# A macaron block with a selective scan: the LayerNorm roots of the mixer split over two engines, the first FFN's statistics and normalisation moved to other slots, x loaded a period sooner, and the beginning in another order

## The chip, the cores and the metric

The kernel runs on one core of a Trainium2 chip. The metric is the device time of one execution in microseconds; the median of three runs is given. A profile is of one execution, and its times are microseconds from the start of its span.

## What is computed

x has 32 sequences of 256 tokens with 128 channels. Three sublayers follow each other, each on a LayerNorm of x:

```python
x = x + 0.5 * ffn(layernorm(x))
x = x + mixer(layernorm(x))
x = x + 0.5 * ffn(layernorm(x))

def ffn(x):                      # E = 8 experts, top 1
    logits = xf @ Wg + bg
    idx = argmax(softmax(logits))
    h = gelu(einsum('th,ehi->tei', xf, W1) + b1)
    y = einsum('tei,eih->teh', h, W2) + b2
    return y[idx]

def mixer(x):                    # selective scan, D_IN = 256, N = 16
    xn = x * rsqrt(mean(x*x) + 1e-6) * norm_w
    x_path, z_path = split(xn @ in_proj_w.T)
    x_path = silu(causal_conv4(x_path))
    dt_x, B, C = split(x_path @ x_proj_w.T)
    dt = softplus(dt_x @ dt_proj_w.T + dt_proj_b)
    h[t] = exp(dt * A) * h[t-1] + dt * x_path * B
    y = sum_n h * C + D * x_path
    return (y * silu(z_path)) @ out_proj_w.T + x
```

The mixer adds its own input, the LayerNorm of x, as a residual, and takes an RMS norm of that same LayerNorm. In the kernel the two norms are one step on the moments: with variance v, the RMS-normed value is (x - mean) times (v (1 + 1e-6) + 1e-11) to the power -1/2, and the residual update is x (1 + r) - mean r, with r = (v + 1e-5) to the power -1/2.

## The kernel before

The tokens are worked on in 16 chunks of 512 (two sequences). A program of 21 iterations, -4 to 16, runs over them as a software pipeline. An iteration has 16 slots, and in iteration i each engine works on several chunks: the state scan of chunk i, the dt path of chunk i+1, the mixer's norm and the end of the first FFN of chunk i+2, the first products of the first FFN of chunk i+3, the statistics of chunk i+4, and the second FFN of chunks i-1 to i-3. The order within an iteration is written by hand in `Plan` tables: for each engine, at which slot a named step is issued (a half or a quarter means behind the slot's units). Iterations 0 to 15 follow `STEADY`; -4 to -1 follow the `FILL` tables, 16 follows `DRAIN`. Each engine runs its own queue in order, and semaphores order the engines among each other.

The state scan has 32 units in a period, two for each slot. For a unit ScalarE writes the decay exp(dt A) into one of three PSUM banks dA0 to dA2 (`make_decay`, L882), GpSimd multiplies dtx by B (`state_bx`, L1253, two units at once), VectorE scans (L1050, L1052), and the product with C is made by VectorE (L1056) or, for half of the units, by GpSimd (`product_c`, L1263). A decay waits until the unit three before it has left its bank. TensorE sums the states (`sum_states`, L656) in the odd slots and in slot 0 of the next iteration. `gated0` and `gated1` on VectorE (L1129) multiply the sums by the gate.

An FFN chunk is a transposed normalised input (`ln_f1`, `ln_f2`), a gate product (`gate_f1`), a one-hot by VectorE (`one_hot`), its transposition (`oh_f1`), eight first products e0 to e7 into the bank PH (two of them into PY), copied out by ScalarE (L830, L827), two batched gelus (L852) with a table load on either side, and eight second products into PY (L644). VectorE adds the result to x (`y_f1`, `y_f2`, L1109).

A norm is made of `norm_stats` on VectorE (`stats_f1`, `stats_f2`, `stats_p`; L1031 to L1037), the root, and the application. In `STEADY` the root is `root_*` on ScalarE: Ln and then Exp with a factor -0.5, from the same table as the decays (L798, L800; for the mixer both roots at once, L807 to L811), while GpSimd's `root_*` negates the mean, waits for ScalarE and makes the shift. In `FILL` GpSimd takes the roots itself as a power (L1211, L1230). `norm_f1` and `norm_f2` on ScalarE apply the norm in four pieces (L789); `norm_p` on GpSimd makes xr (L1241), which TensorE transposes (`ln_p`); `res_p` on ScalarE updates x (L817). SP issues all transfers: `x_in` loads chunk i+4 at slot 5 in `STEADY`, right behind the store of chunk i-3 (`x_out`), and ahead of the store of the B and C rows (`bc`). X has room for eight chunks.

## Time and profile before

| | us |
|---|---|
| median of three runs | 1206.37 (1206.27 to 1208.4) |
| profiled execution | 1208.04 |
| its span | 1206.1 |
| busy in the span: TensorE, GpSimd, VectorE, ScalarE | 1045.0, 1008.1, 1003.7, 924.9 |

The page of the profile gives busy times and the chain of work that ended last; in the order of time that chain shows a beginning up to 94 us, a stretch in which GpSimd's products follow each other up to 190, periods of some 68 us, and from 995 again GpSimd, until an end without a scan from about 1157. To read such a kernel, take one period of it as windows and then as a timeline of each engine: the number in brackets is how long the engine stood before an instruction, and who released it.

### The profile page before, as it was taken

To read this page: it belongs to the slowest core of one execution; us is meant where nothing else is said; L and a number is where in the kernel's file an instruction comes from. 1 tells how busy PE (TensorE), PEld (TensorE's weight loads), DVE (VectorE), ACT (ScalarE), POOL (GpSimd) and SP (SyncE) were. 2 spreads that over 40 slices of the span, in tenths; PEclk is the share of its full clock that TensorE was granted. 3 is DMA by queue.
4 is the path that set the end of the run, shared out by engine and by line. 5 is a ranking of instruction groups with operands and counts; after the bars stand their busy time and mean duration, and the time that the engine had idled before them with its cause. 6 is when DMAs were issued, how large, how long until landed. Compare 5 with 4: busy or idle time off the path is not lost.

```text
span 1206.1 us, 16727 instructions
## 1 busy us (share of the span) xinstructions
PE 1045.0 (87%) x5380; PEld 544.9 (45%) x5380; DVE 1003.7 (83%) x1638; ACT 924.9 (77%) x1440; POOL 1008.1 (84%) x628
## 2 busy tenths in 40 slices
PE   6896959798989999998989999898989997958688
PEld 3452425253535454453534454453544454524246
DVE  2236999998999899898989899899989899999851
ACT  2367687878989797988989797988989787685551
POOL 1129999988999899998999899998999999999920
PEclk9797979898999899998999899998999998988699
DMA  4033434324142424325143424315142423334000
GB/s 104 1 111 146 140 114 143 113 80 168 29 166 98 149 88 159 105 80 185 30 152 111 145 93 140 125 63 189 43 149 98 148 98 138 118 116 140 9 9 18
DMA packets 61751, 130.05 MB, mean 108 GB/s; under 512 B 7552, under 2 KB 28720, under 8 KB 53472
## 3 DMA queue, kind: packets, MB, share of 16 engines
q1 hardware_dynamic: 61664, 128.98, 31.5%
q8 instruction: 43, 0.70, 0.2%
...
## 4 chain that ended last, share of the span: by engine, by line
PE 42%; ACT 17%; POOL 15%; DVE 13%; issue 11%; DMA 1%; SPq 0%; DVEq 0%; POOLq 0%; ACTq 0%
PE PY L644 12%; POOL hb L1253 9%; PE PH L611 9%; PE G L592 6%; DVE dA L1052 5%; ACT hs L852 5%; POOL hb L1263 4%; PE Y L656 4%; DVE hb L1050 3%; ACT dA L882 3%; PE PH L610 3%; ACT hs L830 2%; DVE hb L1056 2%; PE dA L624 2%; PE G L715 1%
## 5 line engine op out<-in xcount | busy, mean ns | idle before, releaser
L1253 POOL TENSOR_TENSOR hb<-dtx_rep,bs 128x1024 f32<-128x1024 f32 x256 | 598.1, 2358 | 17.6 <-PE Y L656 16.1
L882 ACT ACTIVATE dA<-dt_rep,A 128x512 f32<-128x512 f32 x512 | 341.5, 689 | 96.5 <-DVE hb L1056 87.0
L1052 DVE TENSOR_TENSOR_SCAN dA<-dA,hb 128x512 f32<-128x512 f32 x272 | 331.5, 1219 | 8.3 <-DVE oh L1094 3.0
L1050 DVE TENSOR_TENSOR_SCAN hb<-dA,hb 128x512 f32<-128x512 f32 x240 | 279.0, 1206 | 28.2 <-ACT dA L882 28.0
L1263 POOL TENSOR_TENSOR hb<-hb,cs 128x1024 f32<-128x1024 f32 (+1 forms) x128 | 283.1, 2222 | 10.3 <-DVE hb L1050 10.1
L644 PEld LDWEIGHTS PY<-W,hs 128*128 128x128 f32 x2048 | 248.5, 193 | 64.8 <-issue 61.6
L644 PE MATMUL PY<-W,hs 128*128 128x128 f32 x2048 | 260.9, 280 | 0.0
L611 PE MATMUL PH<-xnT,W 128*128 128x512 f32 x396 | 231.8, 668 | 0.0
L1056 DVE TENSOR_TENSOR hb<-dA,cs 128x512 f32<-128x512 f32 x272 | 188.1, 692 | 19.8 <-DVE dA L1052 0.5
L830 ACT COPY hs<-PH 128x512 f32<-128x512 f32 x198 | 115.2, 582 | 95.1 <-PE PH L611 79.5
L656 PE MATMUL Y<-hb,Sel 128*32 128x512 f32 x1024 | 149.7, 655 | 37.3 <-POOL hb L1263 34.8
L610 PE MATMUL PH<-ohT,Lm 24*128 24x512 bf16 x198 | 77.9, 393 | 64.4 <-ACT hs L830 64.4
L852 ACT ACTIVATE hs<-hs 128x2048 f32<-128x2048 f32 x54 | 103.1, 1915 | 0.3
L610 PEld LDWEIGHTS PH<-ohT,Lm 24*128 24x128 bf16 x198 | 18.0, 91 | 157.6 <-ACT hs L830 121.1
L1069 DVE SCALAR_TENSOR_TENSOR xs<-G,Wc,xs 128x506 f32<-128x506 f32 (+2 forms) x96 | 66.7, 737 | 25.7 <-ACT xs L914 23.2
L611 PEld LDWEIGHTS PH<-xnT,W 128*128 128x128 f32 x396 | 60.8, 193 | 46.6 <-issue 46.6
L1279 POOL TENSOR_TENSOR dt<-dt,sp 128x1024 f32<-128x1024 f32 x16 | 37.9, 2367 | 44.8 <-ACT sp L942 44.7
L656 PEld LDWEIGHTS Y<-hb,Sel 128*32 128x32 f32 x1024 | 22.4, 111 | 103.6 <-issue 69.5
L592 PE MATMUL G<-xs,Wxdt 128*128 128x512 f32 x128 | 58.7, 602 | 1.0 <-DVEq L1098 1.0
L789 ACT ACTIVATE xn<-X,shift,rstd 128x128 f32<-128x128 f32 x124 | 50.8, 482 | 5.0 <-POOL shift L1213 5.0
L715 PE MATMUL G<-Wg,xnT 128*128 128x8 f32 x256 | 37.0, 271 | 18.7 <-ACT xnT L778 17.7
L715 PEld LDWEIGHTS G<-Wg,xnT 128*128 128x128 f32 x256 | 34.2, 208 | 37.1 <-ACT xnT L778 37.1
...
## 6 DMA issues: line engine op xcount, KB each, us to landing
...
bs<-bc_rows SPq DMA_DIRECT2D x64, 256.0 KB, 3.8
cs<-bc_rows SPq DMA_DIRECT2D x64, 256.0 KB, 3.7
dtx_rows<-dtx SPq DMA_DIRECT2D x32, 256.0 KB, 2.5
dt_rows<-dt SPq DMA_DIRECT2D x32, 256.0 KB, 2.6
X<-in_x SPq DMA_DIRECT2D x16, 256.0 KB, 3.1
out<-X SPq DMA_DIRECT2D x16, 256.0 KB, 2.4
```

Source lines behind the costliest of these rows:

```text
L610: nc.tensor.matmul(bank[:, :], Lm[:, e, :], ohT[:, w, (it.i0 + off) % 2, :], start=True, stop=False)
L611: nc.tensor.matmul(bank[:, :], W1[:, e, :], xnT[:, w, :], start=False, stop=True).then_inc(full, 1)
L644: last = nc.tensor.matmul(PY[:, P * j:P * (j + 1)], hs[:, w, e, P * j:P * (j + 1)], W2[:, e, :], start=False, stop=e == E - 1 and j == J - 1)
L656: last = nc.tensor.matmul(Y[D32 * g:D32 * (g + 1), :], Sel[:, :], hb[:, (2 * k + g // 2) % HR, g % 2], start=k == 0, stop=q == NQ - 1)
L830: nc.scalar.copy(hs[:, w, e, :], PH[:, :]).then_inc(ph_free, 1)
L852: nc.scalar.activation(a, a, ACT.Gelu).then_inc(gelu[w], 1)
L882: nc.scalar.activation(dA[u % NA][:, :], dt_rep[:, h, g, :], ACT.Exp, scale=A[:, h, g, q:q + 1]).then_inc(decay, 1)
L1050: nc.vector.tensor_tensor_scan(x_in_hb, a, x_in_hb, 0.0, ALU.mult, ALU.add).then_inc(scan, 1)
L1052: nc.vector.tensor_tensor_scan(a, a, x_in_hb, 0.0, ALU.mult, ALU.add).then_inc(scan, 1)
L1056: nc.vector.tensor_tensor(x_in_hb, a, cs[:, q, :], ALU.mult).then_inc(prod, 1)
L1253: nc.gpsimd.tensor_tensor(hb[:, s % HR], dtx_rep[:, h, 2 * m:2 * m + 2, :], bs[:, q, None, :].broadcast_to([P, 2, CH]), ALU.mult).then_inc ...
L1263: nc.gpsimd.tensor_tensor(h_in_hb, h_in_hb, cs[:, q, None, :].broadcast_to([P, n, CH]), ALU.mult) \
```

## The change

`STEADY` and three `FILL` tables get other slots, and the roots of the mixer's norm are divided.

- The second products of the first FFN go from slots 5, 6, 6, 7, 7, 8, 8, 8 to 5, 6, 7, 7, 8, 8, 9, 9. `y_f1` moves from slot 9.5 to 10.0, behind the same `gated0`, and `stats_p` from 10.0 to 10.5, behind units 20 and 21. The copy of first product e5 moves from slot 11 to directly behind the second gelu of the second FFN, ahead of the table load.
- The root for the RMS norm is taken by GpSimd alone (`inverse_root_p`: one operation for the argument and a power), so `norm_p` waits for no other engine. The root for the residual stays with ScalarE, as one Ln and one Exp at slot 11.5 instead of three instructions at 10.5, ahead of the gelus; GpSimd turns it into scale and shift in a new step `res_p` at slot 12.0, for which ScalarE's `res_p` now waits.
- `stats_f1` goes from slot 12 of VectorE to 1.25, `root_f1` from 12.5 to 4.5 on ScalarE and to 6.5 on GpSimd, `norm_f1` from 14.5 to 9.0 on ScalarE. For this x of chunk i+5 is loaded at slot 5, where chunk i+4 was; the load now waits for the store of chunk i-3, issued just before it.
- In the beginning three second products of chunk 0 stand behind the transposes and around the gate of chunk 1, the one-hot copy of chunk 1 ahead of `y_f1` of chunk 0, and the steps of iteration -2 one slot earlier; `res_p` and `norm_f1` there stand behind `taps`. Iteration -1 loads two chunks of x.

```diff
-    w2=[*[(0, e, s, 1, 2) for e, s in experts(5, 6, 6, 7, 7, 8, 8, 8)],
+    w2=[*[(0, e, s, 1, 2) for e, s in experts(5, 6, 7, 7, 8, 8, 9, 9)],
...
-         "ln_f2": 9.5, "root_p": 10.5, "gelu_f2": 10.5, "ln_p": 12.5,
-         "root_f1": 12.5, "res_p": 13.5, "taps": 14.0, "norm_f1": 14.5, "gelu_f1": 15.5},
+         "ln_f2": 9.5, "gelu_f2": 10.5, "root_p": 11.5, "ln_p": 12.5,
+         "res_p": 13.5, "taps": 14.0, "gelu_f1": 15.5},
...
             def scale_residual(it, off):
                 it.wait(act, xr_ready, off, 1, 1)
+                it.wait(act, rooted[2], off, 1, 1)
...
                     if it.has(off):
                         a = hs[:, w, 4 * k:4 * (k + 1)].rearrange("p e t -> p (e t)")
                         nc.scalar.activation(a, a, ACT.Gelu).then_inc(gelu[w], 1)
+                    take_units(it, s, 3 + k)
                     if k == 0:
-                        take_units(it, s, 3)
...
+            def inverse_root_p(it, off):
+                n = roots_before(2, it.i0 + off)
+                it.wait(pool, moments[2], off, 1, 1)
+                it.wait(pool, normed[2], off, 1, 0)
+                nc.gpsimd.tensor_scalar(neg[:, 2, :], mv[:, 2, :, 0], -1.0, 0.0, ALU.mult, ALU.add).then_inc(pool_ln[2], 1)
+                nc.gpsimd.tensor_scalar(var[:, :], mv[:, 2, :, 1], 1.0 + RMS_EPS, RMS_EPS * LN_EPS, ALU.mult, ALU.add) \
+                    .then_inc(pool_ln[2], 1)
+                pool.wait_ge(pool_ln[2], n + 2)
+                nc.gpsimd.tensor_tensor(rms[:, :], var[:, :], half[:, :], ALU.pow).then_inc(pool_ln[2], 1)
+
+            def residual_scale(it, off):
+                n = roots_before(2, it.i0 + off) + 3
                 if root_on_act(2, it.i0 + off):
                     pool.wait_ge(log_root[2], 2 * act_roots(2, it.i0 + off) + 2)
...
+                nc.gpsimd.tensor_scalar(res[:, :], rstd[:, 2, :], 1.0, 1.0, ALU.mult, ALU.add)
+                nc.gpsimd.tensor_tensor(shift[:, 2, :], neg[:, 2, :], rstd[:, 2, :], ALU.mult).then_inc(rooted[2], 1)
...
             def normalize_p(it, off):
-                it.wait(pool, rooted[2], off, 1, 1)
+                pool.wait_ge(pool_ln[2], roots_before(2, it.i0 + off) + 3)
...
-            def load_x(it):
-                dst, src = X[:, it.tiles(4), :], xd[:, J * (it.i0 + 4):J * (it.i0 + 5), :]
-                it.wait(sp_, x_out, 4 - XR, 16, 16)
+            def load_x(it, off):
+                dst, src = X[:, it.tiles(off), :], xd[:, J * (it.i0 + off):J * (it.i0 + off + 1), :]
+                it.wait(sp_, x_out, off - XR, 16, 16)
```

On ScalarE, slots 9 and 10 of a steady iteration (decays 20 to 23 are those into dA2, dA0, dA1, dA2), before:

```order
L830 COPY hs<-PH 128x512
L882 ACTIVATE dA2<-dt_rep,A 128x512
L882 ACTIVATE dA0<-dt_rep,A 128x512
L778 COPY xnT<-G1 128x512
L830 COPY hs<-PH 128x512
L882 ACTIVATE dA1<-dt_rep,A 128x512
L882 ACTIVATE dA2<-dt_rep,A 128x512
L807 ACTIVATE var<-mv,eps 128x4
L808 ACTIVATE var<-mv,eps_p 128x4
L811 ACTIVATE roots<-var 128x8
L852 ACT_TABLE_LOAD
```

and with the change:

```order
L790 ACTIVATE xn<-X,shift,rstd 128x128 x4
L821 COPY hs<-PH 128x512
L873 ACTIVATE dA2<-dt_rep,A 128x512
L873 ACTIVATE dA0<-dt_rep,A 128x512
L779 COPY xnT<-G1 128x512
L821 COPY hs<-PH 128x512
L873 ACTIVATE dA1<-dt_rep,A 128x512
L873 ACTIVATE dA2<-dt_rep,A 128x512
L843 ACT_TABLE_LOAD
```

The normalisation of the first FFN now stands ahead of the copy of first product e1, and nothing stands between decay 23 and the table load of the gelus.

On VectorE, slots 9 to 11 of the same iteration (the scans with dA2 and dA0 behind the addition to x are units 20 and 21), before:

```order
L1129 TENSOR_TENSOR y2<-Y,zs 128x512 [waits summed]
L1109 SCALAR_TENSOR_TENSOR X<-PY,X 128x512 [waits w2_done_f1]
L1031 BN_STATS stat<-X 128x6 [waits moments_p,y_added_f1]
L1031 BN_STATS stat<-X 128x6 x3
L1035 COPY ticket<-ticket 128x1 [waits normed_p,stats_p]
L1037 BN_AGGR mv<-stat 128x2 x4
L1052 SCALAR_TENSOR_TENSOR dA2<-dA2,hb 128x512 [waits bx,decay]
L1056 TENSOR_TENSOR hb<-dA2,cs 128x512 [waits scan,c1_in]
L1050 SCALAR_TENSOR_TENSOR hb<-dA0,hb 128x512 [waits decay]
```

and with the change:

```order
L1119 TENSOR_TENSOR y2<-Y,zs 128x512 [waits summed]
L1099 SCALAR_TENSOR_TENSOR X<-PY,X 128x512 [waits w2_done_f1]
L1042 SCALAR_TENSOR_TENSOR dA2<-dA2,hb 128x512 [waits bx,decay]
L1046 TENSOR_TENSOR hb<-dA2,cs 128x512 [waits scan,c1_in]
L1040 SCALAR_TENSOR_TENSOR hb<-dA0,hb 128x512 [waits decay]
L1021 BN_STATS stat<-X 128x6 [waits moments_p,y_added_f1]
L1021 BN_STATS stat<-X 128x6 x3
L1025 COPY ticket<-ticket 128x1 [waits normed_p,stats_p]
L1027 BN_AGGR mv<-stat 128x2 x4
```

The statistics for the mixer moved behind units 20 and 21; the other statistics, of the first FFN, stood behind the one-hot copy of slot 12 and now stand behind the one-hot steps of slot 1.

On TensorE in the beginning, between the last first products of chunk 0 and the first ones of chunk 1, before:

```order
L644 MATMUL PY<-W2,hs 128x128 x3
L584 MATMUL G0<-Id,xn 128x128 [waits g0_free,normed_f1]
L584 MATMUL G0<-Id,xn 128x128 x3
L715 MATMUL G1<-Wg,xnT 128x8 [waits g1_free,g0_free]
L715 MATMUL G1<-Wg,xnT 128x8 x3
L724 MATMUL G1<-Idb,oh 24x128 [waits g1_free,gate_f1]
L724 MATMUL G1<-Idb,oh 24x128 x3
L623 MATMUL PH<-ohT,Lm 128x512 [waits direct_done,g1_free]
```

and with the change:

```order
L585 MATMUL G0<-Id,xn 128x128 x3
L645 MATMUL PY<-W2,hs 128x128 [waits direct_done]
L645 MATMUL PY<-W2,hs 128x128 x3
L716 MATMUL G1<-Wg,xnT 128x8 [waits g1_free,g0_free]
L716 MATMUL G1<-Wg,xnT 128x8 x3
L645 MATMUL PY<-W2,hs 128x128 [waits direct_done]
L645 MATMUL PY<-W2,hs 128x128 x3
L645 MATMUL PY<-W2,hs 128x128 [waits direct_done]
L645 MATMUL PY<-W2,hs 128x128 x3
L725 MATMUL G1<-Idb,oh 24x128 [waits g1_free,gate_f1]
L725 MATMUL G1<-Idb,oh 24x128 x3
L624 MATMUL PH<-ohT,Lm 128x512 [waits direct_done,g1_free]
```

Three second products, four matmuls each, now stand between the transposes, the gate product and the transposed one-hot.

## Rows read from the trace of the kernel before

**Rows 1.** windows: stretch, length, busy us (count) by engine, TensorE clock, DMA share, GB/s

```profile
40.00:60.00 20.00, 15.86 (x35) 5.85 (x35) 6.10 (x31) 6.03 (x12) 5.98 (x14) 0.66 0.00 0
385.13:453.86 68.73, 63.88 (x337) 33.63 (x337) 62.27 (x102) 59.00 (x93) 62.41 (x39) 0.95 0.35 117
453.86:521.75 67.89, 61.34 (x337) 32.64 (x337) 62.34 (x102) 58.99 (x93) 62.34 (x39) 1.00 0.34 118
```

**Rows 2.** GpSimd's timeline: start us, us, instruction; first and last dt sum

```profile
189.81 2.37 POOL L1279 TENSOR_TENSOR dt<-dt,sp 128x1024 f32<-128x1024 f32 x1
...
1006.60 2.37 POOL L1279 TENSOR_TENSOR dt<-dt,sp 128x1024 f32<-128x1024 f32 x1 [0.87 <-ACT sp L942]
```

**Rows 3.** VectorE's timeline, period of full clock; in brackets idle before, releaser

```profile
472.43 0.69 DVE L1129 TENSOR_TENSOR y<-Y,zs 128x512 f32<-128x512 f32 x1 [0.71 <-PE Y L656]
...
473.76 0.87 DVE L1031 BATCH_NORM_STATS2 stat<-X 128x6 f32<-128x128 f32 x4
...
484.01 0.41 DVE L1105 COPY ohT<-G 24x512 bf16<-24x512 bf16 x1 [0.46 <-PE G L724]
...
486.90 2.34 DVE L1050 TENSOR_TENSOR_SCAN hb<-dA,hb 128x512 f32<-128x512 f32 x2 [1.23 <-ACT dA L882]
...
511.02 3.45 DVE L1050 TENSOR_TENSOR_SCAN hb<-dA,hb 128x512 f32<-128x512 f32 x3 [0.67 <-ACT dA L882]
```

**Rows 4.** timeline of ScalarE in the same period

```profile
471.46 0.59 ACT L830 COPY hs<-PH 128x512 f32<-128x512 f32 x1 [3.12 <-PE PH L611]
...
477.05 0.69 ACT L882 ACTIVATE dA<-dt_rep,A 128x512 f32<-128x512 f32 x1 [2.04 <-DVE hb L1056]
477.68 0.28 ACT L807 ACTIVATE var<-mv,eps 128x4 f32<-128x4 f32 x1
...
478.40 1.28 ACT L852 ACT_TABLE_LOAD   x1
...
489.12 0.29 ACT L798 ACTIVATE vt<-mv,eps 128x4 f32<-128x4 f32 x1
489.44 0.20 ACT L800 ACTIVATE rstd<-vt 128x4 f32<-128x4 f32 x1
...
496.39 1.65 ACT L789 ACTIVATE xn<-X,shift,rstd 128x128 f32<-128x128 f32 x4
...
499.89 0.69 ACT L882 ACTIVATE dA<-dt_rep,A 128x512 f32<-128x512 f32 x1 [1.39 <-DVE hb L1056]
```

**Rows 5.** timeline of TensorE in the same period

```profile
466.72 2.84 PE L644 MATMUL PY<-W,hs 128*128 128x128 f32 x24
...
482.14 0.39 PE L610 MATMUL PH<-ohT,Lm 24*128 24x512 bf16 x1 [2.36 <-ACT hs L830]
```

**Rows 6.** timeline of GpSimd in the same period

```profile
462.15 2.37 POOL L1279 TENSOR_TENSOR dt<-dt,sp 128x1024 f32<-128x1024 f32 x1 [1.25 <-ACT sp L942]
...
478.54 0.19 POOL L1220 TENSOR_SCALAR neg<-mv 128x4 f32<-128x4 f32 x1
...
479.34 1.75 POOL L1241 TENSOR_SCALAR xr<-X,neg,roots 128x128 f32<-128x128 f32 x4
...
489.72 0.20 POOL L1213 TENSOR_TENSOR shift<-neg,rstd 128x4 f32<-128x4 f32 x1 [2.60 <-ACT rstd L800]
```

**Rows 7.** timeline of TensorE in the beginning

```profile
40.50 1.06 PE L715 MATMUL G<-Wg,xnT 128*128 128x8 f32 x8 [0.68 <-ACT xnT L778]
43.21 0.38 PE L724 MATMUL G<-Idb,oh 128*24 128x128 bf16 x4 [1.65 <-DVEq L1098]
45.58 0.60 PE L623 MATMUL PH<-ohT,Lm 24*128 24x512 bf16 x1 [1.99 <-DVE ohT L1105]
46.12 2.08 PE L624 MATMUL PH<-xnT,W 128*128 128x512 f32 x2
```

**Rows 8.** timeline of GpSimd in the beginning: the power of 128x4

```profile
50.61 1.01 POOL L1211 TENSOR_TENSOR rstd<-vt,half 128x4 f32<-128x4 f32 x1
```

**Rows 9.** section 6 of the page, DMA issues: count, KB each, us to landing

```profile
out<-X SPq DMA_DIRECT2D x16, 256.0 KB, 2.4
```

More of the change, by code:

```diff
@@ L225, in roots_before @@
 def roots_before(w, chunk):
-    return sum(1 if root_on_act(w, c) else 4 if w == 2 else 3 for c in range(chunk))
+    return sum((2 if w == 2 else 0) + (1 if root_on_act(w, c) else 3) for c in range(chunk))
 def on_pool(s):
@@ L547, in body @@
                             store_x(it, off)
[L548 to L549 removed]
+                    for t, off in at.get("x_in", ()):
+                        if t == s and it.has(off):
+                            load_x(it, off)
                     if not it.has(1):
```

97 lines of the change are left out of this document (40 added, 57 removed).

## The prediction

> **What bounds the kernel now.** I read the stretches first [rows 1]. In the steady part no engine is full: of 67.89 us in one period VectorE is busy 62.34, GpSimd 62.34, TensorE 61.34 and ScalarE 58.99. Periods come in pairs, one of about 68.7 us with a granted clock of 0.95 and one of 67.9 at 1.00; twelve of them, from the dt sum of GpSimd at 189.81 to the one at 1006.60 [rows 2], take 816.8 us, 68.07 each. So the period is a ring of waits that runs through several engines, and a change is worth what it takes out of that ring. I follow it in the period of full clock. TensorE hands the state sum to VectorE (`gated0`, which waited 0.71 us) [rows 3]; VectorE adds the FFN to x, takes the statistics for the mixer (`stats_p`) and only then scans unit 20. ScalarE waits 2.04 us for that unit's product before it may write decay 23, then computes three small roots, 477.68 to 478.40, loads a table and runs the gelus [rows 4]. TensorE stands 2.36 us until the gelu lets ScalarE free PH [rows 5]; VectorE stands 1.23 us at 486.90 for the next decay [rows 3]. From there VectorE is the late one (ScalarE waits 1.39 us for it at 499.89), until the gelus of the first FFN, after which VectorE waits 0.67 us for decay 3. GpSimd follows with waits of 1.25 and 2.60 us [rows 6].
>
> **Slots 7 to 11.** Of the eight second products of the first FFN, two now stand behind the state sum of slot 9 on TensorE. Three of them take 2.84 us [rows 5], so the sum comes 1.9 us sooner; it is ready before VectorE is, and VectorE's 0.71 goes. The eighth product still ends where the old sum ended, so `y_f1` can start right behind `gated0`, some 0.7 earlier than before. `stats_p` (0.87 + 0.15 + 0.37 us with overlaps, 1.26 from 473.76 to 475.02) moves from ahead of unit 20 to behind unit 21. Unit 20's product is then 0.7 + 1.3 = 2.0 to 2.1 us earlier, and decay 23 with it: I take 2.1, all of the 2.04 plus gaps, since decay 22 is ready then. The roots of ScalarE, 0.72, no longer stand between decay 23 and the gelus. The gelus start 2.8 us earlier. Two things must keep up, and just do: `e5` of TensorE needs the sum of slot 11, for which GpSimd's product ends at 478.5 as before, and its copy now stands ahead of the table load behind the second gelu, which wants it at about 481.8; by the same durations it is ready at 481.5.
>
> **The split roots.** GpSimd computes the root of the normalised input itself: one more small operation (0.19) and one power. I price the power from the beginning, 1.01 us for 128x4 [rows 8], so 1.2 a period, ends 1.0 and 1.6. The neg-to-xr stretch, 0.80 now [rows 6], grows to about 1.7; against it the 2.60 us that GpSimd stood for ScalarE's root_f1 goes, because that root now runs at slot 6.5 behind root_f2. The residual's root is taken by GpSimd at slot 12: it needs ScalarE's Ln and Exp, which stand behind the table reload and two decays; they end about 485.0, GpSimd arrives about 485.3. GpSimd's own ring is the 62.34 busy and 1.2, 63.5 to 64.1 with gaps; it stays under the period. Its transposed input is needed by TensorE 2.7 us after it is ready even so, hence the later `stats_p` costs nothing there.
>
> **First FFN's statistics and normalisation.** `norm_f1`, 1.65 us at 496.39, goes to slot 9, where ScalarE waited 3.12 us at 471.46 for TensorE [rows 4]. That wait is 1.9 shorter by the moved products, so 1.2 of the 1.65 are hidden and 0.4 fall on ScalarE, which has them spare before decay 23. What leaves slot 14 buys nothing in this period, since ScalarE waits for VectorE right behind it (the 1.39). `stats_f1` leaves slot 12, where VectorE waited anyway (0.46 and 1.23) [rows 3], and lands in slot 1.25, 1.26 us ahead of a wait of 0.67: that costs 0.6 on the ring. root_f1 on ScalarE adds 0.49 (0.29 + 0.20) ahead of softplus, so GpSimd's dt sum gains 2.36 instead of 2.85, still more than the ring.
>
> **Sum of a period.** -2.1 - 0.7 + 0.6 = -2.2: 67.9 becomes 65.7. A check from the other side: VectorE waited 0.71, 0.46, 1.23 and 0.67, together 3.1; without them its queue alone asks 64.8, and I leave it 0.9 of waits. The slower of each pair of periods had the lower level of TensorE's clock (1.2 instead of 2.4 GHz in part), and it fell at the 2.4 us stand behind the gelu. That stand shrinks below 0.7. I therefore let all periods run at full clock, so 68.07 becomes 65.7: 12 x 2.37 = **-28.4 us**; bounds 2.2 less by 1.2 (a late `e5`) and the VectorE floor of 64.8, -14 and -39.
>
> The Trainium skill ("TensorE: Matmul & The Clock Gate", Part 1, "What's actually happening") says that "the default state is throttled, and activity releases the throttle". By that rule a denser stream keeps the clock. The trace agrees in that the clock of the period was 0.95 or 1.00 with the same stand of 2.36 us, so a stand of that size can go either way; if the rule gave nothing here, the sum would keep 0.4 us a period.
>
> **The x load.** It is issued one period sooner and now waits for the landing of the store issued just before it, 2.4 us [rows 9]; behind it in SP's queue stands the store of the B and C rows. These rows are read more than 20 us later, so the cost is nil; if that cover were gone it would be 1.5 us a period.
>
> **Beginning.** TensorE idled 0.68 + 1.65 + 1.99 = 4.3 us between the FFN of chunk 0 and that of chunk 1 [rows 7]. Transposes and gate of chunk 1 now lie between the last second products, and the copy of the one-hot stands ahead of `y_f1`; about 0.7 is left, so 3.6 are won. After that stand TensorE ran at the lower clock (0.66 over 40 to 60) [rows 1]: a pair of 2.08 us would be half that. Five pairs and small ones, some 6 us, could come back. Against it ScalarE now does residual and normalisation, twice 1.65 us as in [rows 4], late in that iteration, ahead of the copy of the combined weights for which TensorE waits. The whole comes to between -3.5 and -9; I take **-6**. GpSimd then bounds the first two periods and the one behind the last FFN: +1.2 for two of them that lie outside the twelve, and +0.5 for ScalarE's root ahead of the first dt sum: **+2.9**.
>
> **Total.** -28.4 - 6 + 2.9 = -31.5. The profiled execution took 1208.04 us with a span of 1206.1; its work is that of the median run, 1206.37, within 0.15%, so I subtract from the median: **1174.9**.
>
> **Rivals.** (a) *`e5` ends last.* Sum of slot 11, PH copy, `e5`, its copy: this line has 0.3 us to spare, and it carries GpSimd's product, 16.4 us of work behind the dt sum. If it is 1 us late, the table reload and decay 24 are too, one for one: 12 x 1 = 12, 1187. For it speaks that I have placed some forty waits to 0.1 us; against it that dt itself comes sooner. (b) *The clock still falls* once a period, or in every other one, at a smaller stand: 0.4 to 0.8 a period, 5 to 10 us, 1182. (c) *Only the beginning gains*, because another wait takes the 2.1 us of decay 23, for instance the copy of `e2`, whose matmuls now stand behind two second products; then the 0.6 of slot 1 eats most of the rest: between 1200 and 1206. (d) *Slower.* The same, with the price of VectorE in full: if the gelus start less than 0.6 us sooner, `stats_f1` in slot 1 costs 0.6 a period and gives nothing back in slot 12, which ScalarE limited; and of the 0.49 of root_f1 on ScalarE some 0.3 reach the ring. 12 x 0.9 + 2.9 - 6 = +8: 1214. Against (c) and (d): the 2.04 us is the plainest wait of the period and what stood ahead of it, `stats_p`, is really moved. That the change does not do what it says is no rival here: the order of the instructions shows each move.
>
> **Chances.** Forecast 0.58, (a) 0.15, (b) 0.13, (c) 0.06, (d) 0.08. The range 1167 to 1190 holds the forecast with its bounds, (a) and (b) for the most part. A measurement of this kernel can tell about 0.2% (2.4 us) from no change: faster 0.88, same 0.04, slower 0.08.
>
> **What would show it.** In the steady part: ScalarE's wait for VectorE ahead of decay 23 under 0.6 us; TensorE's stand behind the first gelu under 0.8; no wait of GpSimd ahead of `shift`; a clock of 1.00 in all periods; dt sums 65.7 apart; VectorE no longer idle for decay 3. Right in kind but not in size would be dt sums 64.8 to 67 apart. In the beginning: first products of chunk 1 at 42 instead of 45.6, half as long, and the first `hb` of GpSimd at 88 instead of 94. Wrong would be a period above 67.5, or a new wait of ScalarE for TensorE in slots 10 and 11.

## The result

| | before | after |
|---|---|---|
| median, us | 1206.32 (1205.49 to 1208.40, 4 runs) | 1176.25 (1171.48 to 1177.37, 4 runs) |
| profiled execution | 1208.04 | 1177.37 |
| its span | 1206.1 | 1175.6 |

The ratio is 0.9741, with an interval of 0.9711 to 0.9771: faster by 30 us, where 31.5 were forecast. The two profiled spans are 30.5 us apart, and the sum below is made against that number.

Two rows of the page of the profile after: busy us, share of the span and instructions of each engine, and TensorE's clock in 40 slices of the span, in tenths of full speed:

```profile
PE 1027.6 (87%) x5380; PEld 543.8 (46%) x5380; DVE 1000.0 (85%) x1637; ACT 920.9 (78%) x1426; POOL 1025.1 (87%) x658
...
PEclk9996979799999999999999999999999998979699
```

GpSimd is busy 17 us more than before, by the powers (about 1.0 us for each of 16 chunks), and TensorE 17 us less with the same number of matmuls, 5380: it ran fewer of them at the lower clock (mean clock 0.949 for 0.937).

GpSimd's timeline after, the two dt sums that answer to [rows 2] (start us, us):

```profile
183.25 2.37 POOL L1275 TENSOR_TENSOR dt<-dt,sp 128x1024 f32<-128x1024 f32 x1
...
975.60 2.36 POOL L1275 TENSOR_TENSOR dt<-dt,sp 128x1024 f32<-128x1024 f32 x1 [0.67 <-ACT sp L933]
```

The sixteen dt sums cut the span into pieces that can be compared one by one:

| piece | before | after | difference | forecast |
|---|---|---|---|---|
| start to first dt sum | 81.12 | 72.51 | -8.6 | -6 |
| two intervals bound by GpSimd | 45.82, 62.87 | 46.74, 64.00 | +0.9, +1.1 | with the last one +2.9 |
| twelve periods | 816.79 | 792.35 | -24.4 | -28.4 |
| interval behind them | 62.57 | 63.47 | +0.9 | (in the +2.9) |
| last dt sum to the end | 136.93 | 136.53 | -0.4 | 0 |

Windows after (stretch, length, busy us and count by engine, TensorE's clock, DMA share, GB/s). The first answers to the first of [rows 1], the second is the first of the twelve periods, the others are steady ones:

```profile
40.00:60.00 20.00, 17.30 (x40) 5.75 (x40) 8.02 (x29) 13.16 (x23) 6.45 (x15) 0.91 0.00 1
183.25:252.30 69.05, 60.80 (x280) 27.05 (x273) 61.16 (x101) 52.27 (x87) 63.55 (x42) 0.90 0.32 112
450.05:515.89 65.84, 61.28 (x339) 32.83 (x338) 61.93 (x102) 58.64 (x92) 63.57 (x41) 1.00 0.36 121
581.71:647.77 66.06, 62.48 (x339) 33.59 (x338) 61.92 (x102) 58.95 (x92) 63.53 (x40) 0.97 0.36 121
```

A period of full clock went from 67.89 us [rows 1] to 65.83, where 65.7 was forecast. All but two of the periods behind the first have a clock of 1.00; those two read 0.97 and are 0.2 longer. Before, every other period from the third on read 0.95 and was 0.8 longer. Of the twelve periods only the first got longer: 69.05 against 66.93, with a clock of 0.90 for 0.95.

### The steady period after

ScalarE's timeline after, in the period that begins at 450.05 (start us, us, instruction; in brackets idle before, releaser). It answers to [rows 4]:

```profile
461.89 0.59 ACT L821 COPY hs<-PH 128x512 f32<-128x512 f32 x1 [1.90 <-PE PH L612]
462.37 1.44 ACT L873 ACTIVATE dA<-dt_rep,A 128x512 f32<-128x512 f32 x2
463.83 1.28 ACT L843 ACT_TABLE_LOAD   x1
465.13 1.91 ACT L843 ACTIVATE hs<-hs 128x2048 f32<-128x2048 f32 x1
...
485.31 0.69 ACT L873 ACTIVATE dA<-dt_rep,A 128x512 f32<-128x512 f32 x1 [2.46 <-DVE hb L1046]
```

The wait of 2.04 us before decay 23 is gone: decays 22 and 23 are one group, 1.44 us long where a pair without a wait takes 1.30, and the table load follows directly. What stands ahead of them is new, a wait of 1.90 us for the matmuls of first product e2.

VectorE's timeline after, answering to [rows 3]:

```profile
460.46 0.69 DVE L1099 SCALAR_TENSOR_TENSOR X<-PY,X 128x512 f32<-128x512 f32 x1 [0.27 <-PE PY L645]
...
462.40 0.69 DVE L1046 TENSOR_TENSOR hb<-dA,cs 128x512 f32<-128x512 f32 x1
...
472.32 2.34 DVE L1040 TENSOR_TENSOR_SCAN hb<-dA,hb 128x512 f32<-128x512 f32 x2 [1.14 <-ACT dA L873]
...
497.25 3.42 DVE L1040 TENSOR_TENSOR_SCAN hb<-dA,hb 128x512 f32<-128x512 f32 x3
```

The wait before `y2` (0.71) and the 0.67 for decay 3 are gone, and 1.14 for decay 24 stands where 0.46 and 1.23 stood. Unit 20's product ends at 463.09, just as decay 23 is to start, and the copy of e2 with decay 22 behind it, which waited for TensorE, is done at about 463.0: VectorE and TensorE's matmuls of e2 now hold ScalarE back to within 0.1 us of the same time.

TensorE's timeline after, answering to [rows 5]. The first row is the one behind the copy for which TensorE stood 2.36 us before; the last row stands 38 us later, just behind the silus:

```profile
467.62 0.39 PE L611 MATMUL PH<-ohT,Lm 24*128 24x512 bf16 x1
...
473.93 0.38 PE L642 MATMUL PY<-b_part,ohT 24*128 24x128 bf16 x4 [1.36 <-issue]
...
505.73 0.38 PE L611 MATMUL PH<-ohT,Lm 24*128 24x512 bf16 x1 [0.99 <-ACT hs L821]
```

The stand of 2.36 us behind the first gelu is gone, and so are the slow matmuls that followed it in every other period before (pairs of 2.08 us at 413.94 and 417.02, behind a stand of 2.37 us). In the two periods that still read 0.97 the slow matmuls follow the stand of 1.36 us. Read the last row with the period before it: from such a stand (439.9) to 466.2, for 26 us, TensorE has only one wait, of 0.33 us. GpSimd, answering to [rows 6], has 0.92 before its dt sum at 515.89 and 0.55 for TensorE at 504.48, and none ahead of `shift`; it is busy 63.57 of 65.84.

### The profile page after: what moved, and what is told of

Its sections match the earlier page's. It is cut to its first block, busy times and chain, and to the rows that moved or that the text cites. A ratio compares the mean times of both kernels' runs of the same rounds, so it can differ in the third digit from the quotient of the medians.

```text
span 1175.6 us, 16745 instructions
## 1 busy us (share of the span) xinstructions
PE 1027.6 (87%) x5380; PEld 543.8 (46%) x5380; DVE 1000.0 (85%) x1637; ACT 920.9 (78%) x1426; POOL 1025.1 (87%) x658
## 3 DMA queue, kind: packets, MB, share of 16 engines
q1 hardware_dynamic: 61664, 128.98, 32.1%
## 4 chain that ended last, share of the span: by engine, by line
PE 31%; POOL 20%; DVE 18%; ACT 18%; issue 12%; DMA 1%; SPq 0%; DVEq 0%; POOLq 0%; ACTq 0%
POOL hb L1247 10%; PE PY L645 10%; DVE dA L1042 7%; PE PH L612 6%; POOL hb L1257 6%; DVE hb L1040 5%; ACT dA L873 4%; PE Y L657 4%; ACT hs L843 3%; DVE hb L1046 3%; PE G L593 3%; ACT hs L821 2%; DVE xs L1059 2%; PE PH L611 2%; PE dA L625 1%
## 5 line engine op out<-in xcount | busy, mean ns | idle before, releaser
L645 PEld LDWEIGHTS PY<-W,hs 128*128 128x128 f32 x2048 | 252.3, 195 | 75.5 <-issue 72.3
L645 PE MATMUL PY<-W,hs 128*128 128x128 f32 x2048 | 268.0, 283 | 0.0
L612 PE MATMUL PH<-xnT,W 128*128 128x512 f32 x396 | 226.4, 654 | 0.0
L1021 DVE BATCH_NORM_STATS2 stat<-X 128x6 f32<-128x128 f32 x192 | 41.3, 278 | 12.6 <-DMA X<-in_x 9.9
```

The costliest lines, as they stand in the source:

```text
L612: nc.tensor.matmul(bank[:, :], W1[:, e, :], xnT[:, w, :], start=False, stop=True).then_inc(full, 1)
L645: last = nc.tensor.matmul(PY[:, P * j:P * (j + 1)], hs[:, w, e, P * j:P * (j + 1)], W2[:, e, :], start=False, stop=e == E - 1 and j == J - 1)
```

## The experiments

Each kernel is the changed one but for the edit shown; e5 is the kernel before with a part of the change. Times are the medians, ratios are to runs of the kernel before that were taken on the same chip (medians 1204.60 for e0, e2, e4 and e6, 1206.29 for e1, e3, e5 and e7, 1205.96 for e8 to e11), so between these sets the ratios compare better than the times. "Full clock" is the most common length of a period with a clock of 1.00 (e8 has nearly none, see there), "twelve" the sum of the twelve periods in the profiled execution, of which the first alone differs by up to 4 us with TensorE's clock.

In the text, an e with a number is an experiment, unless it stands with first products, copies, matmuls or a bank, where it is the expert.

| kernel | median, us | ratio, interval | first dt sum | full clock | twelve |
|---|---|---|---|---|---|
| before | 1206.3 | | 81.12 | 67.90 | 816.8 |
| the change | 1176.25 | 0.9741 (0.9711 to 0.9771) | 72.51 | 65.83 | 792.4 |
| e0, the change once more | 1174.63 | 0.9745 (0.9723 to 0.9767) | 73.90 | 65.85 | 789.2 |
| e1, beginning of before | 1183.99 | 0.9804 (0.9775 to 0.9834) | 81.44 | 65.83 | 792.3 |
| e2, first FFN's norm back | 1176.74 | 0.9760 (0.9738 to 0.9783) | 72.62 | 65.52 | 790.8 |
| e3, second products back | 1180.15 | 0.9782 (0.9758 to 0.9806) | 72.42 | 66.27 | 794.1 |
| e4, `stats_p` ahead of unit 20 | 1192.77 | 0.9889 (0.9869 to 0.9909) | 74.77 | 67.20 | 804.8 |
| e5, split roots alone | 1207.80 | 1.0016 (0.9998 to 1.0033) | 75.67 | 67.70 | 818.9 |
| e6, `stats_f1` in slot 12 | 1176.12 | 0.9766 (0.9740 to 0.9791) | 70.56 | 65.84 | 792.7 |
| e7, power taken twice | 1179.29 | 0.9778 (0.9753 to 0.9802) | 74.21 | 65.83 | 791.5 |
| e8, `root_p` ahead of the gelus | 1198.19 | 0.9936 (0.9922 to 0.9950) | 74.37 | (68.04 at 0.97) | 812.8 |
| e9, e5's copy later | 1182.55 | 0.9807 (0.9792 to 0.9823) | 73.37 | 65.76 | 795.5 |
| e10, e7 of the second FFN later too | 1191.84 | 0.9868 (0.9847 to 0.9890) | 74.04 | 67.11 | 808.2 |
| e11, 1.07 us more of TensorE | 1187.24 | 0.9844 (0.9824 to 0.9864) | 72.58 | 66.71 | 799.6 |

### e0: the change once more

No edit.

> The changed kernel once more, on the chip on which the others of this set run, so that they have a neighbour. Every theory expects what was measured: 1171 to 1178 us, ratio 0.971 to 0.977. A steady period of 65.83 us at full clock; where the spread of single executions (1171.5 to 1177.4 so far) comes from TensorE's clock, the granted clock of the shorter ones is the higher one.

Measured 1174.63 us. What was expected of the clock did not come: the longest of its five runs, 1178.54 us, has the same mean clock (0.952) as the profiled one of 1175.55, and the two shortest, 1173.56 and 1173.97, have a lower one (0.950). So the mean clock does not sort the single runs, and what makes their spread stays open. What two profiled executions show is one place of it. The periods of e0 repeat those of the change within 0.3 us but for the first of the twelve, 65.66 us instead of 69.05. TensorE's timeline of the changed kernel there:

```profile
213.82 0.60 PE L611 MATMUL PH<-ohT,Lm 24*128 24x512 bf16 x1 [2.49 <-ACT hs L821]
214.35 2.08 PE L612 MATMUL PH<-xnT,W 128*128 128x512 f32 x2
...
226.73 1.47 PE L716 MATMUL G<-Wg,xnT 128*128 128x8 f32 x8 [2.51 <-ACT xnT L779]
```

and of e0:

```profile
214.36 0.39 PE L611 MATMUL PH<-ohT,Lm 24*128 24x512 bf16 x1 [1.94 <-ACT hs L821]
214.67 1.54 PE L612 MATMUL PH<-xnT,W 128*128 128x512 f32 x2
...
226.28 1.06 PE L716 MATMUL G<-Wg,xnT 128*128 128x8 f32 x8 [2.19 <-ACT xnT L779]
```

The pair of matmuls behind the stand takes 2.08 us at the lower clock and 1.12 at full clock; 1.54 is a mixture. The order of the instructions is the same in both, so it does not decide which of them comes; the stands already differ, 2.49 and 2.51 us in the one against 1.94 and 2.19 in the other. That stretch of the same program is 3.4 us longer at a clock of 0.90 than at 0.95.

The beginning differs as well. TensorE's timeline of the changed kernel:

```profile
20.62 2.00 PE L625 MATMUL dA<-xnT,W 128*128 128x512 f32 x2
...
23.96 0.39 PE L624 MATMUL dA<-ohT,Lm 24*128 24x512 bf16 x1
...
39.40 0.39 PE L624 MATMUL PH<-ohT,Lm 24*128 24x512 bf16 x1 [0.51 <-DVE ohT L1095]
39.71 1.12 PE L625 MATMUL PH<-xnT,W 128*128 128x512 f32 x2
...
56.38 3.67 PE L593 MATMUL G<-xrT,Wz 128*128 128x512 f32 x4 [2.53 <-ACT Wxdt L950]
```

and of e0:

```profile
20.80 2.08 PE L625 MATMUL dA<-xnT,W 128*128 128x512 f32 x2
...
25.35 0.60 PE L624 MATMUL dA<-ohT,Lm 24*128 24x512 bf16 x1
...
41.79 0.38 PE L624 MATMUL PH<-ohT,Lm 24*128 24x512 bf16 x1 [0.51 <-DVE ohT L1095]
...
58.78 1.98 PE L593 MATMUL G<-xrT,Wz 128*128 128x512 f32 x4 [2.53 <-ACT Wxdt L950]
```

In the profiled execution of the change the clock came up about 5 us sooner, at about 22.5 (between 20.6 and 24) instead of 27.5, and the first products of chunk 1 start 2.4 us sooner than in e0; behind the stand of 2.53 us it fell, and four matmuls took 3.67 us instead of 1.98. Either way the stands, 0.51 and 2.53 us, are the same.

### e1: only the beginning undone

```diff
-        w2=[(0, e, 4 + e, 2, 3) for e in range(5)],
-        act={"ln_f1": 0, "norm_f1": 7.5}, ...
+        w2=[(0, e, 4 + e, 2, 3) for e in range(E)],
+        act={"ln_f1": 0, "norm_f1": 11}, ...
...
-        w2=[(0, 5, 0, 0, 2), (0, 6, 0, 1, 2), (0, 7, 0, 1, 2)],
-        dve={"gate_f1": 0, "oh_f1": 0.25, "y_f1": 0.5, "stats_p": 1, ...
+        dve={"gate_f1": 0, "y_f1": 1, "stats_p": 1.5, "oh_f1": 2, ...
```

> The changed kernel with the plans of iterations -4 to -1 as they were before (roots split as in the change), the steady plan new. Theory: the first dt sum of GpSimd came 8.6 us sooner with the change (72.51 instead of 81.12); the second 7.7; all of it is lost: +7 to +9, 1183 to 1185 us. Rival (the periods behind it give part of it back, since the clock falls in another place or a longer wait follows): +2 to +5, 1178 to 1181 us.

Measured 1183.99, 7.7 us above the change, and 7 by the ratios. The steady periods don't notice; the first dt sum is at 81.44 instead of 72.51, 8.9 later. TensorE's timeline of e1, the rows of [rows 7] again:

```profile
45.84 0.60 PE L623 MATMUL PH<-ohT,Lm 24*128 24x512 bf16 x1 [1.99 <-DVE ohT L1094]
46.38 2.08 PE L624 MATMUL PH<-xnT,W 128*128 128x512 f32 x2
```

The stand of 1.99 us and the slow pairs are back. Against the rows of e0, whose clock comes up at the same time as in e1 and before, the new beginning has its first products 3.8 us sooner than before (41.79 for 45.58 [rows 7]) and its pairs at full clock. The price that the prediction named is there as well: TensorE stands 2.53 us for the copy of the combined weights, behind ScalarE's residual and normalisation, where e1 and the kernel before stand 0.68.

### e2 and e6: the first FFN's normalisation

e2 puts statistics, root and normalisation of the first FFN back to slots 12 to 14.5; the early load of x stays.

```diff
-    act={... "root_f2": 4.5, "root_f1": 4.5, "norm_f1": 9.0,
+    act={... "root_f2": 4.5, ... "root_f1": 12.5, ... "norm_f1": 14.5, ...
-    dve={... "stats_f1": 1.25, ...
+    dve={... "stats_f1": 12.0, ...
-    pool={"root_f2": 6.5, "root_f1": 6.5, ...
+    pool={"root_f2": 6.5, ... "root_f1": 12.5}
```

> The changed kernel with the first FFN's statistics, root and normalisation back in slots 12, 12.5 and 14.5 of the steady plan; everything else stays. Theory (the ring of the prediction): the move itself bought nothing, it costs 0.6 us a period in slot 1 of VectorE and puts 0.49 us ahead of softplus; what speaks for it is GpSimd's wait for ScalarE's root at slot 12.5, which comes back but has 2.2 us of room. So 65.2 to 65.8 us a period, 1168 to 1177 us. Rival (the move is the source of the gain, as 1.65 us leave ScalarE ahead of the gelus of the first FFN): 1.2 us or more a period are lost, 1190 us or more.

Measured 1176.74, the time of the change within its interval, with a period of 65.52: the move gained nothing here, and by the period of full clock it costs 0.3 us. Two periods of e2 at a clock of 0.97 take 66.4, so the eleven periods behind the first come to 721.9 us against 723.3. VectorE's timeline of e2 has the wait back that the move had removed, and ScalarE's has the normalisation in slot 14, where ScalarE with the change stands 2.46 us for VectorE (485.31), so that it costs nothing there:

```profile
495.94 3.45 DVE L1040 TENSOR_TENSOR_SCAN hb<-dA,hb 128x512 f32<-128x512 f32 x3 [1.29 <-ACT dA L873]
```

```profile
481.59 1.64 ACT L790 ACTIVATE xn<-X,shift,rstd 128x128 f32<-128x128 f32 x4
```

e6 moves the statistics alone, a period on to slot 12, so that nothing stands in slot 1 and root and normalisation stay where the change has them.

```diff
+                if t == at.get("stats_f1_next") and it.has(5):
+                    it.wait(dve, x_in, 5, 16, 16)
+                    norm_stats(it, 0, 5)
...
-         ... "stats_f1": 1.25, "oh_f2": 12.0, ...
+         ... "stats_f1_next": 12.0, "oh_f2": 12.0, ...
```

> The changed kernel with the statistics of the first FFN taken a quarter of a period earlier still: in slot 12 of the iteration ahead, behind the one-hot copy, where VectorE stands 1.14 us for a decay, for the chunk that was loaded in slot 5. Theory: VectorE loses 1.26 us in slot 1, where it is late, and pays 0.1 in slot 12; the ring shortens by the 0.6 that slot 1 cost and no more, since ScalarE's decay 3 is next: 65.2 a period, 12 x 0.6 = 7, 1166 to 1171 us. Rival (TensorE's copy of e2, for which ScalarE stands 1.90 us, closes the ring, not VectorE): no change, 1174 to 1178 us.

Measured 1176.12 and a period of 65.84: nothing, as the rival has it. The 0.6 us that the prediction charged for slot 1 isn't on the ring. Where the time goes instead is seen in e6's own rows, VectorE first and then TensorE:

```profile
494.53 3.45 DVE L1040 TENSOR_TENSOR_SCAN hb<-dA,hb 128x512 f32<-128x512 f32 x3 [0.67 <-ACT dA L873]
```

```profile
503.82 0.39 PE L611 MATMUL PH<-ohT,Lm 24*128 24x512 bf16 x1 [1.09 <-ACT hs L821]
```

VectorE waits 0.67 us again for decay 3, and TensorE still stands for the copy behind the silus. From the gelus of the first FFN to the copy behind the silus ScalarE has one wait, of 0.52 us for TensorE. So VectorE does not set the pace of slots 15 to 3; it merely fills its wait with the statistics or doesn't. That ScalarE sets it is read from these waits; no run took work from ScalarE there.

### e3, e4 and e8: the three moves of slots 7 to 11, one by one

```diff
-    w2=[*[(0, e, s, 1, 2) for e, s in experts(5, 6, 7, 7, 8, 8, 9, 9)],
+    w2=[*[(0, e, s, 1, 2) for e, s in experts(5, 6, 6, 7, 7, 8, 8, 8)],
```

> The changed kernel with the second products of the first FFN back in slots 5, 6, 6, 7, 7, 8, 8, 8. Theory: the state sum of slot 9 comes 1.9 us later and VectorE waits for it again, 0.7, but y_f1 had to wait for the eighth product anyway (0.27 now), so 0.3 to 0.5 a period: +4 to +6, 1180 to 1182 us. Rival (only the order on VectorE and ScalarE counts): no change, within 2 us of 1176.

Measured 1180.15, with a period of full clock of 66.27, 0.44 more, and 66.4 to 66.5 where the clock read 0.97. ScalarE's timeline of e3 has a wait for VectorE before decay 23 again, and a smaller one for the matmuls of e2 than the 1.90:

```profile
457.08 0.59 ACT L821 COPY hs<-PH 128x512 f32<-128x512 f32 x1 [1.52 <-PE PH L612]
...
461.31 0.69 ACT L873 ACTIVATE dA<-dt_rep,A 128x512 f32<-128x512 f32 x1 [0.68 <-DVE hb L1046]
```

e4:

```diff
-         "y_f1": 10.0, "stats_p": 10.5, ...
+         "y_f1": 10.0, "stats_p": 10.0, ...
```

> The changed kernel with the mixer's statistics back ahead of unit 20 (slot 10.0). Theory: unit 20's product is 1.26 us later, ScalarE stands that long before decay 23, and the gelus, the decays behind them and VectorE follow: +1.3 us a period, 12 x 1.3 = 15, 1190 us (1187 to 1193). Rival (ScalarE's wait of 1.90 us for e2 has taken the place of that wait, so unit 20 has room): +0 to +4, 1175 to 1180 us.

Measured 1192.77 and 67.20: 1.37 us a period for a step of 1.26 us. In e4's timelines decay 23 waits 1.41 us for VectorE again, and VectorE later waits 2.38 us for decay 24, 1.24 more than with the change:

```profile
467.55 0.69 ACT L873 ACTIVATE dA<-dt_rep,A 128x512 f32<-128x512 f32 x1 [1.41 <-DVE hb L1046]
```

```profile
476.75 2.34 DVE L1040 TENSOR_TENSOR_SCAN hb<-dA,hb 128x512 f32<-128x512 f32 x2 [2.38 <-ACT dA L873]
```

e8:

```diff
-         "ln_f2": 9.5, "gelu_f2": 10.5, "root_p": 11.5, "ln_p": 12.5,
+         "ln_f2": 9.5, "gelu_f2": 10.5, "root_p": 10.5, "ln_p": 12.5,
```

Within slot 10.5 the root is issued ahead of the gelus.

> The change, but ScalarE's Ln and Exp for the residual stand again ahead of the gelus of the second FFN (slot 10.5) instead of behind them (11.5). In the profile after the change the argument of that root is ready at 465.46, where VectorE ends stats_p, and decay 23 leaves ScalarE free at 463.8. Theory (the root only had to leave this place because stats_p had moved behind unit 21; the two moves need each other): ScalarE waits 1.6 us there and works 0.5, so a period is 2.1 longer, 67.9 instead of 65.83, and the time is 12 to 14 periods longer: +25 to +29, 1200 to 1205. Rival (the later gelus have room): only the 0.5 us of work counts, period 66.3, +6 us.

Measured 1198.19 and 68.04, 2.21 us a period, longer than the period before. ScalarE's timeline of e8:

```profile
469.68 0.30 ACT L799 ACTIVATE vt<-mv,eps 128x4 f32<-128x4 f32 x1 [1.68 <-DVE mv L1027]
```

1.68 of wait and 0.5 of work. All but two of e8's periods read 0.97 or 0.98, with a pair of 2.08 us behind a new stand of TensorE of 2.10 us; what that costs is not told apart from the 2.2, which wait and work alone make up. The time, 1198.19, came out just under the expected 1200 to 1205. So the root had to leave this place because `stats_p` went behind unit 21, and the two moves are one.

### e5: the split alone

The tables of before, with the divided root in them.

> The kernel before with the split roots alone: GpSimd takes the root for xr by a power, ScalarE one Ln and one Exp at 10.5 instead of three instructions, GpSimd's residual scale right behind xr; all other slots as before. Theory: ScalarE gains 0.2 us a period ahead of the gelus, GpSimd pays 1.2 where it has 5 us of waits: -2 to +2 in the steady part, +1.2 in each of three GpSimd-bound periods: 1206 to 1211 us. Rival (the split is what frees the ring, as xr no longer waits for ScalarE): 1195 us or less.

Measured 1207.80 in twelve runs, ratio 1.0016 with an interval of 0.9998 to 1.0033: no gain. A ScalarE with one instruction less ahead of the gelus takes 0.2 us off a period of full clock (67.70 for 67.90), and the powers give it back where GpSimd is the bound (63.98 and 63.51 for 62.87 and 62.57). The split pays only by what it makes possible: `norm_p` needs no ScalarE, so ScalarE's root may stand behind the gelus.

e5 shows one thing more. Its beginning is that of before, and yet its first dt sum stands at 75.67, where before has 81.12 and e1 81.44. TensorE's timeline of e5:

```profile
18.26 1.63 PE L624 MATMUL dA<-xnT,W 128*128 128x512 f32 x2
...
41.97 0.60 PE L623 MATMUL PH<-ohT,Lm 24*128 24x512 bf16 x1 [1.93 <-DVE ohT L1094]
...
47.18 1.13 PE L624 MATMUL dA<-xnT,W 128*128 128x512 f32 x2
```

Here the clock came up before 20 us, and behind the stand of 1.93 us it was back at 47, not at about 58 as before. So the old order has its first products of chunk 1 at 42 too when the clock is early, and the 5.8 us between e5 and e1, which has the same tables in the beginning and the split as well, are not the work of the order.

### e7: the price of the power

```diff
+                nc.gpsimd.tensor_tensor(spare[:, :], var[:, :], half[:, :], ALU.pow)
                 nc.gpsimd.tensor_tensor(rms[:, :], var[:, :], half[:, :], ALU.pow).then_inc(pool_ln[2], 1)
```

> The changed kernel with the power of the split root done twice on GpSimd, the first into a spare tile: the disputed cost by itself, 1.01 us more for GpSimd in each period. Theory: GpSimd is busy 63.6 of 65.8 us and waits 0.91 and 0.55 in a steady period, so the steady part does not move; the three or four periods that GpSimd bounds pay 1.1 each: +3 to +5, 1179 to 1181 us. Rival (GpSimd is part of the ring): +1.0 in every one of 16 periods, 1190 us or more.

Measured 1179.29, and GpSimd's timeline of e7 has the two powers:

```profile
468.47 1.02 POOL L1215 TENSOR_TENSOR spare<-var,half 128x4 f32<-128x4 f32 x1
...
469.47 1.01 POOL L1216 TENSOR_TENSOR rms<-var,half 128x4 f32<-128x4 f32 x1
```

The steady periods stay at 65.83: GpSimd's 63.57 has room for one more, and its wait before the dt sum is 0.73 us. Two of the three intervals that were taken for GpSimd's grow by 0.95 and 0.97 (64.95 and 64.44 for 64.00 and 63.47); the first does not (46.26 for 46.74).

### e9 and e10: two attempts at something better

VectorE's largest wait after the change is the 1.14 us for decay 24, which stands behind both gelus and three copies. e9 moves one copy:

```diff
-                                              (11, 1, 10, 4), (12, 0, 12, 0), (12, 2, 13, 0))],
+                                              (11, 1, 11, 2), (12, 0, 12, 0), (12, 2, 13, 0))],
```

> The change, but the copy of first product e5 stands behind decays 24 and 25 on ScalarE instead of ahead of the table load behind the second gelu. Theory (what closes the ring now is ScalarE's stretch from decay 23 over both gelus to decay 24, for which VectorE waits 1.14 us; TensorE is close behind): that stretch is 0.5 to 0.6 us shorter, VectorE's 1.14 falls to about 0.6, period 65.3, 12 to 14 x 0.5 = -6 to -8 us, 1168. The price is that TensorE gets e7's bank some 1.6 us later; it stood 1.36 us right behind. Rival (TensorE closes the ring in slots 9 to 12, and needs that copy where the change put it): period 65.8 to 66.1, -0 to +4 us. Second rival (the diff was right about the place): the clock falls at the longer stand of TensorE, +5.

Measured 1182.55, 6 us worse than the change. VectorE's timeline of e9, then TensorE's, then two windows:

```profile
470.66 2.34 DVE L1040 TENSOR_TENSOR_SCAN hb<-dA,hb 128x512 f32<-128x512 f32 x2 [0.67 <-ACT dA L873]
...
473.29 1.23 DVE L1042 TENSOR_TENSOR_SCAN dA<-dA,hb 128x512 f32<-128x512 f32 x1 [0.28 <-ACT dA L873]
```

```profile
471.81 0.38 PE L611 MATMUL PH<-ohT,Lm 24*128 24x512 bf16 x1 [1.79 <-ACT hs L821]
```

```profile
382.41:448.87 66.46, 62.44 (x339) 33.75 (x338) 62.25 (x102) 58.79 (x92) 63.53 (x41) 0.97 0.35 120
448.87:514.62 65.75, 61.15 (x338) 32.75 (x337) 62.02 (x102) 58.68 (x92) 63.55 (x41) 1.00 0.35 122
```

The wait of VectorE fell as expected, and the period of full clock by 0.08 only: 0.28 of the 0.47 that left ahead of decay 24 came back two units later, and the rest wasn't on the ring. What came with it is TensorE's stand of 1.79 us ahead of first product e7, and a lower clock: five of the twelve periods read 0.97 and one 0.95, and four of them take 66.45 to 66.48, where the change has two of 66.06. The last of the twelve, at 0.95, takes 66.59 for 64.36. The eleven periods behind the first come to 728.0 us for 723.3; the 1.6 us that are left of the 6.3 are less than the single runs of one kernel differ by. The expected 1168 was missed, and the second rival on record, the clock, was nearest.

e10 adds:

```diff
-                                           (1, 0, 0, 2, -2), (2, 0, 2, 1, -2), (3, 0, 3, 0, -2), (4, 1, 4, 1, -2))]],
+                                           (1, 0, 0, 2, -2), (2, 0, 2, 1, -2), (3, 0, 3, 0, -2), (5, 1, 5, 2, -2))]],
```

> As e9_e5_copy_behind, and first product e7 of the second FFN stands on TensorE behind the dt products, at slot 5, instead of ahead of them at slot 4, where it waited 0.99 us for a copy that stands behind the silus; its copy on ScalarE goes from slot 4 to 5. Theory (TensorE's dense stretch from there to the last second product of slot 9 is part of the ring, as y_f1 waits 0.27 us for it): the stretch starts up to 1 us sooner, y_f1's 0.27 goes, and softplus may come up to 0.6 sooner; another -0.3 a period, 65.0, 1164 to 1166. Rival (VectorE, which has no wait from 497 to 460 of the next period, is the bound there): no more than e9 gives, within 2 us of it. On the other side: the state sum or the second products of slot 5 are late behind e7, +0.5 a period over e9.

Measured 1191.84, with periods of 67.11, where 65.0 was expected and the worst case on record was 0.5 above e9. ScalarE's timeline of e10, then TensorE's:

```profile
448.78 0.59 ACT L821 COPY hs<-PH 128x512 f32<-128x512 f32 x1 [1.66 <-PE PH L612]
```

```profile
442.29 1.98 PE L593 MATMUL G<-xs,Wxdt 128*128 128x512 f32 x4 [0.47 <-ACT bcT L779]
...
446.08 0.33 PE L725 MATMUL G<-Idb,oh 128*24 128x128 bf16 x3 [1.80 <-ACT sp L927]
```

The stand of 0.99 us was no loss: without first product e7 there, TensorE runs into the banks that ScalarE has not emptied yet, 0.47 and 1.80 us. And ScalarE waits 1.66 us for first product e7 in the middle of the softplus, ahead of decays and of the dt sum.

### e11: does TensorE's dense stretch count?

```diff
+                        if w == 1 and it.plan is STEADY:
+                            it.wait_free(pe, g_free, f"ln_f{w + 1}")
+                            for j in range(2 * J):
+                                nc.tensor.transpose(G[BANK[f"ln_f{w + 1}"]][:, P * (j % J):P * (j % J + 1)], xn[:, w, j % J, :], Id[:, :])
                         transposes(it, f"ln_f{w + 1}", lambda j: xn[:, w, j, :])
```

> The change, with the four transposes of the second FFN's input made three times over into the same bank in slot 9 of every steady iteration: 1.07 us more of TensorE (2 x 0.53), nothing else. They stand ahead of the last second products of the first FFN and of first product e2. Theory (copy of e2, y_f1 and by them unit 20 and decay 23 hang on TensorE, which has no idle time from 507 to 466 of the next period): the 1.07 us comes through in full, period 66.8 to 66.9, +13 to +15 us, 1189 to 1191, and ScalarE's wait for e2 grows from 1.90 to 2.9. Rival (VectorE's queue is the bound, TensorE only looks dense): 0.2 to 0.3 us a period, +3 to +4 us.

Measured 1187.24, with periods of 66.71: 0.88 us of the 1.07 come through. VectorE's timeline of e11:

```profile
461.15 0.69 DVE L1103 SCALAR_TENSOR_TENSOR X<-PY,X 128x512 f32<-128x512 f32 x1 [1.14 <-PE PY L645]
```

The wait of 0.27 became 1.14, 0.87 more, and the period is longer by just that. That is a little less than the expected 66.8 to 66.9, and ScalarE's wait for the matmuls of e2 went only from 1.90 to 2.05 (2.9 was expected), since 0.61 us of waiting had come in ahead of the copy of e1. So the end of TensorE's queue in slot 9 is part of the ring of the changed kernel; that the queue is, back to the silus, follows from its only wait on the way, 0.33 us.

## Why the prediction was right, point by point

**Slots 7 to 11: right in place, 0.7 too large.** -2.1 and -0.7 were forecast for decay 23 and for the roots, -2.8 together. The period of full clock lost 2.07 in all, and with nothing for slot 1 (below) that is what these moves brought. e3 and e4 give back 0.4 and 1.4 of it, e8 shows why the root had to go, and e5 that the split brings 0.2 by itself.

**The ring's new closing link: wrong.** The prediction had VectorE as the late one from slot 13 on, and its check of the period (64.8 and 0.9 of waits) went by VectorE's queue. Up to the gelus of the first FFN VectorE is the late one (ScalarE waits 2.46 us for it at 485.31); behind them it is not. After the change the ring runs from ScalarE's silus over the copy behind them into 26 us of TensorE with one wait of 0.33, from there at the same time into `y_f1` on VectorE (0.27) and into the copy of e2 on ScalarE (1.90), over decay 23 and both gelus to decay 24, and back over VectorE and ScalarE. e11 shows the TensorE part of it in slot 9, and e6 that VectorE is not on it in slots 15 to 3; the rest of the path is read from waits.

**`stats_f1` in slot 1: the term was mis-sized.** +0.6 was charged, e6 gives 0.0. The step rested on the 0.67 us before decay 3 [rows 3]: that wait was taken for the only room that the statistics have. It reappears in e6 with no gain for the period, so it was idle time of an engine that wasn't the bound. The move as a whole, which the title of the change names, gains nothing: without it (e2) the period of full clock is 0.3 us shorter and the time the same.

**The named sign of failure came, and was none.** "A new wait of ScalarE for TensorE in slots 10 and 11" stands there with 1.90 us, for the copy of e2, and rival (c) named that copy. It did not eat the gain, because it ends just when VectorE's product for decay 23 does. A wait that takes the place of another tells only that the two were within reach of each other. e4 shows that decay 23 still hangs on VectorE's order: with the statistics back ahead of unit 20 the wait for the matmuls of e2 stays 1.90 and the period is 1.37 longer.

**The period: 65.83 against 65.7.** That the errors are small is in part chance: 0.6 too much for slot 1 stands against a gain in slots 7 to 11 of 2.1 instead of 2.8. By the rows it is TensorE's matmuls of e2 and `y_f1`'s 0.27 that cut the gain short; no run took work from TensorE to show it.

**The clock.** All periods at full clock were forecast. Nine of the eleven periods behind the first are, and two read 0.97 and cost 0.2 each. The stand of 2.36 us behind the gelu, which was blamed for it, is gone; a shorter one, 1.36 us, has the slow matmuls of those two periods behind it. Where the clock comes up and falls differs between executions of one program, by the rows of e0. The Trainium skill, "TensorE: Matmul & The Clock Gate", Part 1, says of the start of a kernel that the same one has a different number of slow matmuls from run to run, and the trace agrees: the clock comes up between 20.6 and 24 us in one execution and later than 25.4 in the other.

**Twelve periods: -24.4 against -28.4.** 3.35 of the 4.0 that are missing lie in the first of them, 69.05 instead of 65.7. The prediction multiplied the mean of twelve by twelve; it did not look at the first one, which has fewer matmuls (280 for 339 in the windows) and longer stands of TensorE. e0 has 65.66 there and -27.6 for the twelve, and that execution is the forecast to within 1 us. That is luck too: in the profiles of other kernels with this beginning and nearly this period it is 68.88 (e2), 65.93 (e3), 69.65 (e6) and 68.38 (e7), so the long form is the more frequent one. Such a difference is over half of the spread of the change's single runs, 1171.5 to 1177.4.

**Beginning: -8.6 against -6.** Right in its parts, of which the prediction gave the first as 3.6: in e0 the first products of chunk 1 start 3.8 us sooner, at 41.79 (42 was forecast). Five pairs and their small ones at full clock give 5.3 more, and the stand of 2.53 for the combined weights, 0.68 before, takes 1.9: together -7.2, e0's first dt sum at 73.90. The prediction took less, since it let the price of that stand be larger. But the 5.3 are not sure to be the order's: in e5 the old order has the clock back after one slow pair and a part of a second, and is 1.8 us faster than before from the first products of chunk 1 to the first dt sum (33.7 us for 35.5, where e0 takes 32.1). So the order is worth some 5.4 to 7.2 us here, by these profiles, and e1 gives 7 by the runs. What the profiled execution has beyond it, 1.4 us, is the clock that came up sooner, 2.4, less 1.0 that is left of the four matmuls at the lower one. The first `hb` of GpSimd stands at 86.41, for the forecast 88.

**GpSimd's price: right in sum, by luck in its parts.** +2.9 was forecast as 1.2 for two intervals and 0.5 for a root on ScalarE ahead of the first dt sum. In the sum above it is three intervals, +0.9, +1.1 and +0.9, and no root of ScalarE stands ahead of the first dt sum: in the beginning GpSimd still takes that root itself. e7 shows 1.0 us for one further power in two of the three intervals and nothing in the periods that GpSimd does not bound.

**Rivals.** (a), a late e5: its copy has no wait at 469.70. (b), the clock: in part, 3.4 us in the first period of the profiled execution and 0.2 in each of two others. (c) and (d) needed the gain of decay 23 to vanish, and e4 shows that it did not. No version beat the change; the experiments e2 and e6 equal it, e2 with less moved.
